# Gated blocks in DRAM in natural row order, low parts taken from PSUM, and the order of V and of the first modulation product, in a two-layer conditional residual kernel on one Trainium2 core

## The reference

```
# layer 0: adapter picked by the batch's language, then a layer norm
h  = relu(x @ W1[lang] + b1[lang])                      # 512 -> 128
x1 = x + layernorm(x + h @ W2[lang] + b2[lang]) * gamma0 + beta0
# layer 1, on x1
ctx    = causal_ema(x1, tau_ctx)                        # scan over tokens
g      = x1 * sigmoid([x1, ctx] @ Wg.T + bg)
m      = 0.5 + sigmoid(gelu(x1 @ Wn1.T + bn1) @ Wn2.T + bn2)      # 8 modulations per token
traces = causal_ema(g * m[d], tau[d])  for d in 0..7
temporal = sum_d softmax(blend)[d] * traces[d]
gate   = sigmoid(temporal @ Wtemp.T + btemp)
soma   = gelu(x1 @ Wsoma.T + bsoma)
out    = x1 + layernorm((soma * gate) @ Wout.T) * gamma1 + beta1
```

## Time and profile before

| | |
|---|---|
| median of 3 runs | 1514.78 us (1514.3 to 1514.91) |
| profiled execution, own time | 1509.55 us |
| its span | 1507.8 us |
| PE, PEld | 1372.3 us (91%), 977.2 us (65%) |
| DVE | 1019.1 us (68%) |
| ACT | 515.4 us (34%) |
| POOL | 393.2 us (26%) |
| DMA queue 1 | 66050 packets, 184.97 MB, 42.3% of 16 engines |
| mean granted TensorE clock | 0.975 of full |

### The profile page before, as it was taken

The page is one execution under the profiler, slowest core; times in us unless marked ns, Lnnn a source line. Parts: engine busy times, 40 slices in busy tenths (PEclk is TensorE's granted clock), DMA queues, the critical chain, the costliest instruction groups (busy, mean ns, idle before and its releaser), DMA issues.

```text
span 1507.8 us, 19538 instructions
## 1 busy us (share of the span) xinstructions
PE 1372.3 (91%) x7836; PEld 977.2 (65%) x7836; DVE 1019.1 (68%) x1493; ACT 515.4 (34%) x812; POOL 393.2 (26%) x295
## 2 busy tenths in 40 slices
PE   2689989999999999999998998999999999998985
PEld 1566858576685766757576685757758576685744
DVE  6868676685667857577684767668576685767363
ACT  2324333242333424333242423424233332433323
POOL 4314123041330504123041422304133050411103
PEclk8799999999999999999999999999999999999999
DMA  7354351825427063361715526172541806334150
GB/s 240 112 144 143 95 161 60 203 77 138 141 61 226 35 165 109 107 194 49 201 44 144 170 71 181 57 193 93 134 146 58 228 29 168 113 99 125 49 144 32
DMA packets 66140, 186.22 MB, mean 124 GB/s; under 512 B 9090, under 2 KB 13826, under 8 KB 53762
## 3 DMA queue, kind: packets, MB, share of 16 engines
q1 hardware_dynamic: 66050, 184.97, 42.3%
HBM read 134.61 MB, written 50.33 MB: 123 GB/s over the span
## 4 chain that ended last, share of the span: by engine, by line
DVE 24%; DMA 21%; PE 19%; issue 13%; ACT 12%; SPq 3%; POOL 3%; POOLq 0%; DVEq 0%
DMA g_spans<-g_f 12%; PE ring L861 10%; DMA grep<-g_spans 9%; DVE U L763 7%; PE Tp L1014 4%; PE Tp L1005 4%; SPq L326 3%; ACT U L482 2%; DVE x L701 2%; DVE V L706 2%; DVE U L645 2%; DVE seq_lo L651 2%; DVE soma_r L659 2%; PE ring L854 2%; ACT g_r L448 2%
## 5 line engine op out<-in xcount | busy, mean ns | idle before, releaser
L763 DVE TENSOR_TENSOR U<-grep,w_qs 128x1024 f32<-128x1024 f32 x256 | 301.9, 1219 | 102.8 <-DMA grep<-g_spans 102.6
L385 POOL TENSOR_TENSOR x<-grep,b_row 128x512 f32<-128x512 f32 x64 | 81.9, 1312 | 668.1 <-DMA grep<-in_x 668.1
L1005 PE MATMUL Tp<-U,Arep 128*32 128x256 f32 x2048 | 153.0, 404 | 14.8 <-DVE U L763 13.8
L768 DVE TENSOR_TENSOR g_f<-ring,bg_row 128x512 f32<-128x512 f32 x64 | 44.2, 690 | 156.7 <-PE ring L861 156.6
L394 POOL TENSOR_TENSOR grep<-grep,beta_row 128x512 f32<-128x512 f32 x64 | 93.6, 1494 | 179.9 <-DMA grep<-x_tiles 179.9
L490 ACT ACTIVATE g_f<-g_f 128x512 f32<-128x512 f32 x64 | 40.5, 632 | 254.9 <-DVE g_f L768 254.7
L494 ACT ACTIVATE T_sb_f<-Tp 128x512 f32<-128x512 f32 x64 | 38.2, 598 | 260.7 <-PE Tp L1014 260.7
L1005 PEld LDWEIGHTS Tp<-U,Arep 128*32 128x32 f32 x2048 | 54.0, 112 | 105.0 <-DVE U L763 47.9
L861 PE MATMUL ring<-Wout_hi,g_r 128*128 128x512 f32 x256 | 102.2, 399 | 19.5 <-DVE soma_r L659 19.5
L861 PE MATMUL ring<-seq_hi,Wtemp_hi 128*128 128x512 f32 x256 | 106.8, 417 | 8.5 <-DVE seq_lo L651 8.5
L1014 PE MATMUL Tp<-V,Epow 128*128 128x512 f32 x128 | 76.7, 683 | 41.0 <-DVE V L778 41.0
(11 more groups left out here) (151 smaller groups left out, 2865.5 us busy)
## 6 DMA issues: line engine op xcount, KB each, us to landing
grep<-g_spans SPq DMA_DIRECT2D x256, 256.0 KB, 5.0
grep<-in_xc SPq DMA_DIRECT2D x16, 1024.0 KB, 7.2
grep<-in_x SPq DMA_DIRECT2D x16, 1024.0 KB, 9.0
x_tiles<-x SPq DMA_DIRECT2D x16, 1024.0 KB, 7.6
g_spans<-g_f SPq DMA_DIRECT2D x64, 256.0 KB
grep<-x_tiles SPq DMA_DIRECT2D x16, 1024.0 KB, 4.8
out<-U SPq DMA_DIRECT2D x64, 256.0 KB, 2.0
gamma_row<-in_g SPq DMA_DIRECT2D x9, 256.0 KB, 7.3
```

Of the source, the lines that this page charges most:

```text
L385: nc.gpsimd.tensor_tensor(new[:, b, :], x_t[:, b, :], b2_row[:, :], ALU.add).then_inc(xb2_ready, 1)
L763: V_.tensor_tensor(U[:, (n + 2) % 4, :, :], grep[b % 2][:, :, at], w_qs[:, hh, at].unsqueeze(1).to_broadcast([P, NI, HC]), ALU.mult).then_ ...
L768: V_.tensor_tensor(g[:, b, :], bank_of("wg", k, b)[:, :], bg_row[:, :], ALU.add).then_inc(pre_ready, 1)
L1005: last = nc.tensor.matmul(Tp[b % 2][i * L:(i + 1) * L, at], Arep[:, b * NI + i, hh, :], U[:, (n + 2) % 4, i, :], start=(hh == 0 and c == 0 ...
```

## The change

1. `g_dram` is `[NB, P, C]`: a block is kept as its 128 rows in natural order. `store_spans` writes it without rearrangement; `repeat_spans` reads it with the rearranged view, so that each partition of `grep` gets four rows of 2 KB that lie 32 rows apart.
2. SP issues store b and repeat b block by block.
3. The gated soma and the adapter's relu are left in their PSUM banks; the high and low parts are taken from there. The banks are free once the low part is done.
4. The first modulation product is taken out of the ring, put into `Tp[0]`, and moved ahead of the previous tile's output projection on TensorE; its gelu on ScalarE is moved ahead of the output copies.
5. On DVE `products(0, 1, 0)` goes ahead of `gate_logits(3)`, and `gated(3)` and V (`span_states`) come after it and `products(0, 1, 1)`, V ahead of `products(1, 0, 0)`. On TensorE the span states come between the two within-span groups of block 0.

```
-        g_dram = nc.dram_tensor("g_spans", [NB, L, NI * C], F, kind="Internal").ap()
+        g_dram = nc.dram_tensor("g_blocks", [NB, P, C], F, kind="Internal").ap()
...
-                order += [("n1", k, 0), ("soma", k, 0)] + [("wg", k, b) for b in range(NB)]
+                order += [("soma", k, 0)] + [("wg", k, b) for b in range(NB)]
...
-        read_by = {"h": h_ready, "temp": sg_ready, "n1": h1_ready, "soma": soma_ready, "trx": ema_ready,
+        read_by = {"h": hidlo_ready, "temp": somalo_ready, "soma": soma_ready, "trx": ema_ready,
...
+        inner_bank = Tp[0]
...
-                    sp.dma_start(g_dram[b].rearrange("s (i c) -> i s c", i=NI), g[:, b, :]).then_inc(g_stored[b], 16)
+                    sp.dma_start(g_dram[b], g[:, b, :]).then_inc(g_stored[b], 16)
...
-                        sp.dma_start(grep[b % 2][q * L:(q + 1) * L, :, :].rearrange("p i c -> p (i c)"),
-                                     g_dram[b]).then_inc(grep_in[b % 2], 16)
+                        sp.dma_start(grep[b % 2][q * L:(q + 1) * L, :, :],
+                                     g_dram[b].rearrange("(i s) c -> s i c", i=NI)).then_inc(grep_in[b % 2], 16)
...
-                    store_spans(0)
-                    repeat_spans(0)
-                    store_spans(1)
-                    store_spans(2)
-                    repeat_spans(1)
-                    store_spans(3)
-                    repeat_spans(2)
-                    repeat_spans(3)
+                    for b in range(NB):
+                        store_spans(b)
+                        repeat_spans(b)
...
-                    nc.scalar.activation(soma_hi[:, e, :], soma[:, e, :], ACT.Identity).then_inc(somahi_ready, 1)
+                    nc.scalar.activation(soma_hi[:, e, :], ps[:, :], ACT.Identity).then_inc(somahi_ready, 1)
...
-                    nc.scalar.activation(hid[:, :], bank_of("h", k + 1, 0)[:, :], ACT.Relu, bias=b1_col).then_inc(h_ready, 1)
+                    ps = bank_of("h", k + 1, 0)
+                    nc.scalar.activation(ps[:, :], ps[:, :], ACT.Relu, bias=b1_col).then_inc(h_ready, 1)
...
+                    act.wait_ge(full["n1"], upto(1, k, 0))
+                    nc.scalar.activation(hid[:, :], inner_bank[:, :], ACT.Gelu, bias=col[:, 0:1]).then_inc(h1_ready, 1)
                 if has_prev:
                     for b in range(NB):
                         act.wait_ge(full["out"], upto(4, k - 1, b))
...
-                    V_.tensor_tensor(soma[:, e, :], bank_of("temp", k - 1, e)[:, :], soma[:, e, :],
-                                     ALU.mult).then_inc(sg_ready, 1)
+                    ps = bank_of("temp", k - 1, e)
+                    V_.tensor_tensor(ps[:, :], ps[:, :], soma[:, e, :], ALU.mult).then_inc(sg_ready, 1)
                     dve.wait_ge(somahi_ready, upto(4, k - 1, e))
-                    V_.tensor_tensor(soma_lo[:, e, :], soma[:, e, :], soma_hi[:, e, :].bitcast(F),
+                    V_.tensor_tensor(soma_lo[:, e, :], ps[:, :], soma_hi[:, e, :].bitcast(F),
...
                     products(0, 0, 1)
+                    products(0, 1, 0)
                     gate_logits(3)
-                    products(0, 1, 0)
+                    products(0, 1, 1)
                     gated(3)
-                    products(0, 1, 1)
+                    span_states()
                     products(1, 0, 0)
-                    span_states()
...
+                if has_cur:
+
+                    pe.wait_ge(ema_ready, upto(4, k, NC - 1))
+                    if k == 0:
+                        pe.wait_ge(split_lo[0], 1)
+                    pe.wait_ge(x1lo_ready, upto(4, k, NC - 1))
+                    split_product(inner_bank[:, :], lambda a, n: Wn1[a][:, n, :], lambda a, n: x1T[a][:, n, :],
+                                  NC).then_inc(full["n1"], 1)
                 if has_prev:
                     pe.wait_ge(somalo_ready, upto(4, k - 1, NC - 1))
...
                     within_spans(0, 0)
+                    span_states()
                     within_spans(0, 1)
-                    span_states()
```

More of the change, by code:

```diff
@@ L457, in slot @@
                     act.wait_ge(full["h"], upto(1, k + 1, 0))
-                    nc.scalar.activation(hid[:, :], bank_of("h", k + 1, 0)[:, :], ACT.Relu, bias=b1_col).then_inc(h_ready, 1)
+                    ps = bank_of("h", k + 1, 0)
+                    nc.scalar.activation(ps[:, :], ps[:, :], ACT.Relu, bias=b1_col).then_inc(h_ready, 1)
                     act.wait_ge(h_ready, upto(1, k + 1, 0))
-                    nc.scalar.activation(hid_hi[:, :], hid[:, :], ACT.Identity).then_inc(hidhi_ready, 1)
+                    nc.scalar.activation(hid_hi[:, :], ps[:, :], ACT.Identity).then_inc(hidhi_ready, 1)
                 if has_prev:
@@ L483, in slot @@
                 if has_cur:
-                    act.wait_ge(full["n1"], upto(1, k, 0))
-                    nc.scalar.activation(hid[:, :], bank_of("n1", k, 0)[:, :], ACT.Gelu, bias=col[:, 0:1]).then_inc(h1_ready, 1)
                     soma_gelu(0)
@@ L675, in slot @@
                     dve.wait_ge(hidhi_ready, upto(1, k + 1, 0))
-                    V_.tensor_tensor(hid_lo[:, :], hid[:, :], hid_hi[:, :].bitcast(F), ALU.subtract).then_inc(hidlo_ready, 1)
+                    V_.tensor_tensor(hid_lo[:, :], bank_of("h", k + 1, 0)[:, :], hid_hi[:, :].bitcast(F), ALU.subtract).then_inc(hidlo_ready, 1)
                 if k == 0:
@@ L1029, in slot @@
                 if has_cur:
-                    ps = free_bank(pe, "n1", k, 0)
-                    pe.wait_ge(x1lo_ready, upto(4, k, NC - 1))
-                    if k == 0:
-                        pe.wait_ge(split_lo[0], 1)
-                    split_product(ps[:, :], lambda a, n: Wn1[a][:, n, :], lambda a, n: x1T[a][:, n, :], NC).then_inc(full["n1"], 1)
                     if k == 0:
```

## The result

The changed kernel takes 1423.47 us in the median of 4 runs (1422.44 to 1424.65), the kernel before 1514.54 beside it. The ratio is 0.9402, 95% interval 0.9386 to 0.9418: 91 us faster. The profiled execution took 1424.65 us with a span of 1422.9; before it was 1509.55 and 1507.8, so that the two traces differ by 84.9 us and the medians by 91.

The account below looks back on a forecast made before the run. The prediction took the DMA as the full resource in the back half, with a slow store of g delaying grep and V. 62 + 19.5 = 81 us, less 1, gave 1514.78 - 80 = 1435 us; range 1418 to 1474.

Parts of the forecast that it names:

- The bound: Back half of a tile: DMA is the full resource; block 0's 5.85 us store makes grep[1], and so V, late.
- Part 1: Layout of g in DRAM and order on SP: store 2.2 us instead of 5.85, 2 KB pieces 0 extra per block.
- Part 2: V ahead of block 1: back half 25.2 us instead of 30.4 (even tile) and 27.7 (odd), 62 us in all.
- Rival (d): DMA store of g does not spread, grep[1] still comes at about 822.3: 1474 us, chance 0.10.
- Part 3: Low parts from PSUM on DVE: 0.69 us each, 0.38 less for each of 64, 24 us of DVE in all.
- Part 4: First modulation product, moved before the output projection, covers TensorE's wait for the soma low part: 19.5 us.
- The sum: Whole kernel: 62 + 19.5 = 81 us, less 1 for the first tile: 80 us gained, 1435 us.
- (b): Repeats of g become somewhat slower: 0.7 us on each gives back 30 us, 1465 us, chance 0.11.
- (c): 2 KB pieces cost each repeat the full 2.4 us, grep[1] for block 3 late: 59 us slower, 1574, chance 0.05.

Follow-up runs that it names:

- the row order alone: The kernel before with only the natural row order of g in DRAM (g_dram, store and repeat views): 1451.96 us, ratio 0.9617.
- V alone: The kernel before with only V's new place on DVE and the span states' new place on TensorE: 1502.92 us, ratio 0.9976.
- the four stores of 32 rows: The kernel after with the old 8 KB rows in DRAM, each block stored by four DMAs of 32 rows: 1444.18 us, ratio 0.9606.

## Why the prediction was right, step by step

**The bound.** Right. The late grep was what TensorE waited for through V, and it was late because of the store: with the row order alone the wait for V and 4.1 us of each back half go. The reading that the DMA is the full resource in the back half was too strong: after the change its share there is 0.88, hardly less than 0.90, and yet 74% of the chain that ended last is TensorE.

**Part 1.** The store was taken at 2.2 us and measured 2.17. The extra of the 2 KB pieces was taken at 0 of a range up to 2.4, and none can be seen. The repeats' 6.9 us are 6.5 to 6.9 by their landings. The window of a repeat in the earlier trace rows was not of a repeat alone: SP issued store 1 at 717.93, inside it. The conclusion drawn from it held all the same. The warning that the order on SP would cost 4 us a tile with the long store was right: it cost 67 / 16 = 4.2, the clock's part included.

**Part 2.** Back halves of 25.2 were forecast and are 24.8 and 25.3. The sum for this term, 62 us, measured 63.7. On the even tile's clock, with its first within-span matmul at 0, V was forecast at 2.1 and started at 2.0; DVE's wait for it was forecast at 2.3 and is 2.18; the clock stayed at 1.00. The mean rests on tiles 7 and 8, read as odd and even. What tells the long back halves from the short ones is not parity but the fall of the clock, which came in seven even tiles and in three odd ones; the means are 29.3 and 28.4 us, not 30.4 and 27.7. That the two tiles average 29.05, close to the 28.85 of all, is partly luck. The two losses in it, the wait and the low clock behind it, were both named, and they make up 61 of the 63.7 us.

The forecast put the layout, the order on SP and V's place into one sum and did not say who earns it. The runs say that the layout does, all of it. V's new place is worth 0.2 us in the median tile beside the new order on SP (0.4 in the mean) and nothing beside the old one, for 24.78 us with old V and old order is no more than 24.83 with new V and old order. Rival (d) had V alone right in kind, a gain far below the 41 us, and too large in size: 1.3 us a tile was forecast, 0.73 came, and most of that was clock.

**Part 3.** The low part costs 692 ns (mean) against 1070, the product into PSUM 691 against 679. By form, on DVE, beside the earlier trace rows:

```profile
L770 DVE TENSOR_TENSOR g_f<-g_f,x 128x512 f32<-128x512 f32 x64 | 56.0, 875 | 30.6 <-ACT g_f L488 30.6
...
L657 DVE TENSOR_TENSOR soma_r<-ring,g_r 128x512 fp32r<-128x512 f32 x64 | 44.3, 692 | 42.5 <-ACT g_r L445 42.5
L655 DVE TENSOR_TENSOR ring<-ring,soma_f 128x512 f32<-128x512 f32 x64 | 44.2, 691 | 29.1 <-ACT ring L443 29.1
...
L671 DVE TENSOR_TENSOR W_r<-W_f,W_hi 128x512 fp32r<-128x512 f32 x8 | 8.7, 1084 | 0.0
```

So 24.2 us of DVE were saved at the low part, as forecast, and 0.7 lost at the product. But DVE's total fell only from 1019.1 to 1010.4: `gated` went from 46.1 to 56.0 us and the weights' low part from 5.5 to 8.7. The saving was not on the path either way, since undoing this part costs the tiles nothing.

**Part 4.** 19.5 us were counted and the front gave 22.5, so the number is close in part by luck. Of the 19.5, 3.2 stayed: 2.8 of them belong to slot 16, which has no modulation product to move. Against that, 4.46 us come from the last front alone, where there is no next tile's adapter to stand between the temporal gate and the output projection. The output projection starts there 14.2 us after the first temporal product as before (14.3), but the 2.7 us of the modulation product now lie in the wait, and the fall of the clock behind the wait (1.6 us, in the row above) is gone; the forecast had no term for that. In the other tiles the moved product gets 1.30 us each by itself, and part 3 by itself 0.86. The forecast that it covers the wait "even where part 3 gives nothing" is the run with the old low parts. The chain from the first logits to store 0 did not move, as forecast: store 0 is issued 756.79 - 753.70 = 3.09 us after the logits, before 798.43 - 795.36 = 3.07.

**The sum.** 80 us forecast, 84.9 between the spans, 91 between the medians, 1435 against 1423.5. The two terms are right within 3 us each, with the luck told above. The rest of the difference to 91 is that the profiled execution before was 5 us below its median and the one after 1.2 above. The kernel before varies with its clock: in the later rounds 1492.05 us came with a granted clock of 0.986 and 1523.80 us with 0.966, where the executions of the kernel after lie at 0.987 to 0.988.

**The rivals.** (b) and (c) fell with the landings of the repeats; (d) fell with the store. The mechanism of (b) and (c), an extra on each block that adds up over the four, is seen with the store in the place of the repeat in the old layout under the new order.

## What to carry to other kernels

When a short transfer gates a longer one, look at the DMA share while the short one runs. Here a share of 0.23, beside an output store of the same size that landed in 2.0 us, told that the shape and not the size was the price, and one view in DRAM was worth more than every reordering around it. Ask of each reordering whether it still works when its neighbour edit is missing: store-then-repeat block by block is free with a 2 us store and costs 4 us a tile with a 6 us store. Filling an engine's idle time can give nothing: the product ahead of V did, since DVE then waited for TensorE and ScalarE instead; with the two low parts moved as well 12 us came. And a wait can cost more than its length: at ten of the 16 waits for V the granted clock fell, which added about half as much again.

## What the runs showed of the hardware

**A store onto an outer dimension of four.** The 256 KB store of g ran at a DMA share of 0.23 and 58 GB/s when its DRAM side had an outer dimension of 4 (5.85 us), and at 0.54 and 202 GB/s as 128 plain rows with nothing beside it (2.0 us). The places in DRAM differed too, but they are not the price: the four stores of 32 rows write to the old places and land a block in 3.03 us, 1.7 of them taken by their issues. The engines can be counted: for each store of block 0 in the trace before, the DMA updates the store's semaphore 5 times (80 for 16 stores), in tile 8 once 0.94 us after the issue and four times between 5.25 and 5.83 us; in the trace after 16 times (256), in tile 8 between 1.96 and 2.15 us. The Trainium skill (DMA: Bandwidth & Descriptors, "Why a DMA increments its semaphore by 16 and not by 1") says that the slowest dimension of both sides sets the number of engines, 4 against 16; the shares and the updates agree with it.

**DVE and GpSimd get in each other's way, and the place moves.** In the kernel after, GpSimd adds x1 to the result here,

```profile
751.03 5.18 POOL L409 TENSOR_TENSOR U<-U,grep 128x512 f32<-128x512 f32 x4 [0.84 <-ACT U L482]
```

and DVE's `gated(0)`, which now starts 1.64 us after the first logits began (755.34 - 753.70) where it took 2.35 before, runs into it:

```profile
755.34 1.42 DVE L770 TENSOR_TENSOR g_f<-g_f,x 128x512 f32<-128x512 f32 x1 [0.66 <-ACT g_f L488]
```

1.42 us instead of 0.69. Its two inputs are in SBUF. Over the kernel after, the 15 `gated` that overlap a GpSimd instruction take 1.48 us in the mean and the other 49 0.69. The soma low part tells the same: before, with two inputs in SBUF, 39 of its 64 overlap GpSimd and take 1.31 us in the mean, the others 0.69; now, with one input in PSUM, 43 overlap it and all 64 take 691 to 694 ns. The Trainium skill (SBUF — State Buffer, "Who interferes with whom") says just this, that a DVE instruction with two SBUF inputs contends with a GpSimd instruction that reads SBUF and one with a single SBUF input does not; these times agree.
